# Two conditioned sequence blocks on one core: ranking, residual, last unit, DMA queue, and a product that starts on a copy of another in its PSUM bank

## The chip, the cores and the metric

The kernel runs on one core of a Trainium2 chip. The metric is device time in microseconds of one launch. The engines that matter are TensorE (PE in the profile), VectorE (DVE), ScalarE (ACT), GpSimd (POOL) and SyncE, whose queue (SPq) issues nearly all DMAs.

## The reference, cut to what matters

The input x is 32 batches of 64 tokens with 512 features, float32. Two layers follow each other; each is a block of attention and two MLPs, and then an adapter whose weights are chosen by the batch's role (one of three).

```python
attn = softmax(q @ k.T * 512**-0.5)            # q = x @ Wq, k = x @ Wk, per batch
attn_out = (attn @ v) @ Wp + bp                # v = x @ Wv
cms_out = gelu(attn_out @ cW1 + cb1) @ cW2 + cb2 + one_hot(code)      # first MLP, 512 -> 2048 -> 512
modifier = gelu(concat(attn_out, cms_out) @ mW1 + mb1) @ mW2 + mb2    # second MLP, 1024 -> 2048 -> 512
x = clip(x + cms_out + modifier, 0, 1)
u = gelu(x @ W_down[role] + b_down[role]) @ W_up[role] + b_up[role]    # adapter, 512 -> 256 -> 512
x = layernorm(x + u) * gamma[role] + beta[role]
```

## The kernel before

**Numbers.** Each float32 operand of a product is split into a high and a low part (ScalarE rounds the high part, VectorE subtracts it to get the low one) and a product is three matmuls (`product`, L543). "Split" below means this pair of operations; `h_hi`, `h_lo`, `s_lo` and the like are its semaphores.

**Passes.** Two halves of 16 batches (1024 tokens) times two layers are four passes p = 0 to 3. A pass is: attention for two blocks of 512 tokens, 16 units of MLP work (`mlps`: units 0 to 7 are the first MLP, 8 to 15 the second, each of 256 hidden features), and eight adapter tiles of 128 tokens. Every engine has its own program in a fixed order; semaphores tie them.

**The start.** The weights Wq Wk.T and Wv Wp of both layers are fused first: four products n = 0 to 3 in two sets of four PSUM banks, with `operands(n)` (split of the inputs) and `results(n)` (split of the product). Results are also stored to DRAM by SyncE, and `results(n)` on ScalarE waits for the store of n - 2 (`fuse_stored`) before it writes its buffer again. Between operands(1) and operands(2) VectorE runs `rank_batches` (L1177 on), some 40 tiny dependent steps that sort the batches so that tiles hold one role; SyncE waits for it (L340), reads the order from SBUF into registers and loads x batch by batch (`load_x`). Meanwhile GpSimd splits the bias rows in four operations on 4 x 2304 elements (L482 to L488).

**A unit** (`term`, `down`, `hidden`). Units 0 and 8 are plain: four blocks. The other 14 multiply 2 x 2 blocks with seven products P1 to P7. PE's order in unit u is P1, P5, P6, the down products of unit u - 1 for token block 0, P2, P7, the down products for block 1, P4, P3. P1 and P2 add up in `bank_a` (ps[0]), P6, P7 and P4 in `bank_b` (ps[1]), P5 and P3 in `bank_c`. ScalarE copies P1 to SBUF (`copy_p1`, L990), and VectorE adds it to what stands in bank_b after P6 (`make_u2`), after P7 (`make_z22`, which also adds P5) and after P4 (`make_z21`); `make_z12` adds P3. `hidden` takes the activation of the four results (H00, H10, H01, H11) in two ScalarE passes, and VectorE makes the low part. `add` (L1394) adds the down products to `acc`.

**The last unit** (15) also loads and splits the adapter's weights: `adapter_part` for down, `up_part` for up, in three roles each. VectorE's order ends: H11, up_part 0, up_part 1, z12, H01, the added token piece, the four `add` of block 0, adapter_part 2, clips.

**An adapter tile i.** VectorE clips acc (`clip`, two buffers xc), both engines split it, PE multiplies with the down weights and then turns the clipped tile into PSUM as the residual (both in `front`, the latter L803), after a wait for `normalise` of tile i - 3, since u_bank has three banks:

```python
for i in range(TILES):
    if i + 2 < TILES: r[i + 2] = front(p, half, i + 2)     # down product, then wait yn_done, then residual
    if i + 1 < TILES: turn_h(p, i + 1)
    if layer == 0 and 2 <= i < TILES - 1: turn_back(p, half, i - 2)
    adapter_up(p, half, i, r.pop(i))
```

VectorE's loop is: row_stats(i - 1), clip(i + 3), split_x(i + 3), normalise(i - 1), split_h(i + 1). GpSimd makes 1 / std (L523), then multiplies by gamma and adds beta (L526, L528). In layer 0, PE turns the tile back (`turn_back`, L840) for the next pass; in layer 1 SyncE stores it. SyncE's loop is: gains of tile i + 2 (two DMAs, each with a register load of the role), store of tile i (two DMAs, each with a register load of the batch), and between the halves three loads of x (each with a register load).

**Between passes.** Attention starts with four products per block (j = 0 to 3). Before a layer-1 pass, tile 5 is turned back ahead of them, tile 6 after j = 1, tile 7 after j = 3.

## Time and profile before

| | us |
|---|---|
| median of 3 runs | 2183.42 (2183.08 to 2183.86) |
| the profiled execution | 2183.24 |
| its span | 2181.4 |
| PE busy | 2094.2 (96%) |
| VectorE busy | 1417.4 (65%) |
| ScalarE busy | 864.6 (40%) |
| GpSimd busy | 378.1 (17%) |
| matmul weights loading (PEld) | 1729.3 |
| mean granted TensorE clock | 0.987 |

The table is read like this: the profiled execution is as long as the timed ones, so sums can be made against it. PE is nearly always busy, the others are not, and so the questions are where PE stands idle, who ends that, and where its clock is granted below 1.00.

### The profile page before, as it was taken

The numbers are of one execution on the slowest core, as the hardware profiler recorded it, in microseconds if no ns is written. First come the engines' busy times: TensorE is split into PE (matmuls) and PEld (weight loads), VectorE is DVE, ScalarE is ACT, GpSimd is POOL, SyncE is SP. The second block draws the span as 40 slices with busy tenths as digits, with TensorE's granted clock in tenths as the row PEclk, the third lists the DMA queues.
The fourth block names the chain that finished last, engine by engine and source line by source line (L and its number), as shares of the span: only waits on it lengthen the run. The fifth ranks groups of instructions, "written<-read, shape, count | busy, mean of one in ns | idle before, by whom it ended". The sixth has DMA issues, their size and how long they took to land.

```text
span 2181.4 us, 27070 instructions
## 1 busy us (share of the span) xinstructions
PE 2094.2 (96%) x9640; PEld 1729.3 (79%) x9640; DVE 1417.4 (65%) x2228; ACT 864.6 (40%) x1492; POOL 378.1 (17%) x348
## 2 busy tenths in 40 slices
PE   5999999999799999999889999999989999999996
PEld 4888888887688888888768888888867888888874
DVE  8577786557558777556646777765555777865563
ACT  4454453333245444333325444333324544433331
POOL 3011112210311102111130110212122111112204
PEclk8999999999999999999999999999999999999998
DMA  4501111223320121112451111111332012111123
GB/s 174 234 30 58 49 63 58 68 68 97 131 78 30 58 80 37 68 68 68 152 157 39 49 59 66 65 60 52 107 121 102 20 49 68 68 46 60 65 92 97
DMA packets 42402, 169.74 MB, mean 78 GB/s; under 512 B 5648, under 2 KB 9744, under 8 KB 34832
## 3 DMA queue, kind: packets, MB, share of 16 engines
q1 hardware_dynamic: 42272, 168.02, 22.7%
q8 instruction: 80, 1.31, 0.2%
q14 instruction: 50, 0.41, 0.1%
HBM read 146.99 MB, written 21.01 MB: 77 GB/s over the span
## 4 chain that ended last, share of the span: by engine, by line
PE 87%; DVE 6%; SPq 2%; issue 2%; ACT 1%; POOL 1%; DMA 1%; DVEq 0%; ACTq 0%; POOLq 0%
PE psum L543 80%; PE psum L828 1%; PE psum L640 1%; DVE acc L1394 1%; PE psum L618 1%; DVE yt L1541 1%; PE psum L803 1%; PE psum L795 1%; DVE xz L1146 1%; DVE stats L1526 1%; DVE fpart L1146 0%; ACT xz L1095 0%; DVE wup L1146 0%; PE psum L831 0%; POOL yt L526 0%
## 5 line engine op out<-in xcount | busy, mean ns | idle before, releaser
L543 PE MATMUL psum<-hs,wd 128*128 128x512 f32 x3072 | 718.2, 389 | 5.6 <-DVE acc L1394 5.6
L543 PEld LDWEIGHTS psum<-hs,wd 128*128 128x128 f32 x3072 | 576.1, 188 | 128.1 <-DVE acc L1394 7.3
L1394 DVE TENSOR_TENSOR acc<-psum,acc 128x512 f32<-128x512 f32 x448 | 291.0, 682 | 101.4 <-PE psum L543 101.2
L543 PE MATMUL psum<-cop,wsm 128*128 128x512 f32 x1416 | 354.7, 389 | 0.0
L543 PE MATMUL psum<-aop,wsm 128*128 128x512 f32 x1320 | 332.9, 389 | 0.0
L543 PE MATMUL psum<-aop,wsc 128*128 128x512 f32 x1320 | 310.7, 389 | 0.0
L543 PEld LDWEIGHTS psum<-cop,wsm 128*128 128x128 f32 x1416 | 265.8, 188 | 55.1
L543 PEld LDWEIGHTS psum<-aop,wsm 128*128 128x128 f32 x1320 | 247.8, 188 | 51.4
L543 PEld LDWEIGHTS psum<-aop,wsc 128*128 128x128 f32 x1320 | 247.5, 188 | 51.3
L1008 ACT ACTIVATE hs<-psum,bias 128x512 fp32r<-128x512 f32 x88 | 60.8, 691 | 445.4 <-PE psum L543 445.3
L1146 DVE TENSOR_TENSOR hs<-zt,hs 128x512 fp32r<-128x512 f32 x256 | 179.9, 703 | 85.5 <-ACT zt L1009 85.5
L1008 ACT ACTIVATE hs<-zt,bias 128x512 fp32r<-128x512 f32 x168 | 120.5, 717 | 229.1 <-DVE zt L1376 173.1
L1369 DVE TENSOR_TENSOR zt<-psum,zt 128x512 f32<-128x512 f32 x56 | 38.7, 692 | 184.5 <-PE psum L543 184.5
L1009 ACT ACTIVATE zt<-zt,bias 128x512 f32<-128x512 f32 x168 | 119.0, 708 | 0.0
L497 POOL TENSOR_TENSOR comb<-w1m 128x512 f32<-128x512 f32 x28 | 36.2, 1292 | 476.7 <-DMA w1m<-m_in 476.7
L1146 DVE TENSOR_TENSOR wsm<-w1m,wsm 128x512 fp32r<-128x512 f32 x156 | 107.9, 711 | 0.0
L543 PE MATMUL psum<-fw,xs 128*128 128x512 f32 x384 | 97.2, 406 | 4.7 <-DVE tq L1146 3.4
L978 ACT ACTIVATE wsm<-w1m 128x512 fp32r<-128x512 f32 x156 | 93.9, 623 | 3.7 <-POOL w1m L504 3.7
L501 POOL TENSOR_TENSOR comb<-comb,w1m 128x512 f32<-128x512 f32 x28 | 48.9, 1746 | 249.6 <-DVE wsm L1146 249.6
L497 POOL TENSOR_TENSOR comb<-w1c 128x256 f32<-128x256 f32 x28 | 20.7, 740 | 408.8 <-DMA w1c<-c_in 408.8
L543 PE MATMUL psum<-xs,fw 128*128 128x512 f32 x384 | 90.7, 395 | 0.4 <-DVE xs L1146 0.4
L543 PEld LDWEIGHTS psum<-fw,xs 128*128 128x128 f32 x384 | 73.1, 195 | 20.8 <-DVE tq L1146 3.9
(169 smaller groups left out, 2439.6 us busy)
## 6 DMA issues: line engine op xcount, KB each, us to landing
w1m<-m_in SPq DMA_DIRECT2D x32, 1024.0 KB, 4.9
w1c<-c_in SPq DMA_DIRECT2D x32, 512.0 KB, 3.5
w<-c_in SPq DMA_DIRECT2D x32, 512.0 KB, 3.5
w<-m_in SPq DMA_DIRECT2D x32, 512.0 KB, 3.5
gains<-roles_in SPq DMA_DIRECT2D x64, 256.0 KB, 3.6
fw<-fused SPq DMA_DIRECT2D x6, 2048.0 KB, 10.0
fused<-fw SPq DMA_DIRECT2D x4, 2048.0 KB, 8.2
xmid<-x SPq DMA_DIRECT2D x4, 2048.0 KB, 6.7
```

What stands on the lines that cost most here:

```text
L497: nc.gpsimd.tensor_tensor(st, w_block(u, 1, 0), w_block(u, 1, 1), ALU.add).then_inc(s1_made, 1)
L501: nc.gpsimd.tensor_tensor(st, st, w_block(u, 0, 0), ALU.subtract).then_inc(s2_made, 1)
L543: mm = nc.tensor.matmul(out, lhs(a), rhs(b), start=(start and n == 0), stop=(stop and n == total - 1), skip_group_check=reopened)
L618: nc.tensor.matmul(out, tq[:, j // 2, HI, j % 2, i * P:(i + 1) * P], xs[:, :, j, tile], start=(j == 0), stop=False)
L640: nc.tensor.matmul(out, val[:, HI, v_cols], val[:, :, p_cols], start=True, stop=False)
L795: nc.tensor.matmul(out, tokens, wdn_flat[:, bass.ds(role * (2 * KC * BN) + (c * KC + k) * BN, BN)], start=(b == 0 and k == 0 and a == c), ...
L978: nc.scalar.activation(slot(u, i)[:, HI, :], w_source(u, i), ACT.Copy).then_inc(s_hi[i], 1)
L1008: nc.scalar.activation(hs[:, b, HI, m, :], h_source(h, u), ACT.Gelu, bias=b1)
L1009: nc.scalar.activation(h_raw(h), h_source(h, u), ACT.Gelu, bias=b1).then_inc(h_hi[h], 1)
L1146: return nc.vector.tensor_tensor(out, a, hi.bitcast(F32), ALU.subtract)
L1369: nc.vector.tensor_tensor(zt[:, 2, :], bank_b()[:, :], zt[:, 0, :], ALU.add).then_inc(u3_done, 1)
L1394: nc.vector.tensor_tensor(dst, d_out[o][:, :], dst, ALU.add).then_inc(acc_done, 1)
```

## The change

It has five parts. (1) Start: the bias rows are laid out on 128 partitions and split in two operations instead of four; the ids are loaded from ScalarE's queue; ranking has 37 steps, of which ten run before operands(0) and 27 before operands(2); the one-hot table is made after results(3). (2) Adapter tiles: `residual` leaves `front` and runs behind turn_h of its own tile; the clip has a third buffer; tile 5 is turned back after attention's j = 0, tile 6 after j = 2. (3) Last unit: up_part 1 and 2 and the last adds move behind the first clips and splits. (4) SyncE: one gains DMA for a tile of one role; the order of the batches is read into registers once per half and kept. (5) In 7-product units ScalarE copies P1 into bank_b itself, P6 adds to it there, P4's result is read from bank_b directly; ScalarE copies P5 and the sum after P6 to SBUF; of VectorE's sums one before P4 and one after P3 remain. In the plain unit of the first MLP, H01 has bank ps[1] instead of ps[4].

The diff, cut to its core:

```diff
-RANKED = 40
+RANKED = 37
...
+        xct2 = at("xct2", [P, KC, P], F32, HS + 14)
...
-        xc = [xct[:, s, :, :] for s in range(2)]
+        xc = [xct[:, 0, :, :], xct[:, 1, :, :], xct2[:, :, :]]
...
-        back_bank = [ps[3], ps[4]] * (TILES // 2 - 1) + [ps[6], ps[7]]
+        back_bank = [ps[3], ps[4], ps[3], ps[4], ps[3], ps[6], ps[7], ps[6]]
...
-            return {H00: ps[0], H10: ps[6], H01: ps[1], H11: ps[7]} if kind else {H00: ps[2], H10: ps[3], H01: ps[4], H11: ps[5]}
+            return {H00: ps[0], H10: ps[6], H01: ps[1], H11: ps[7]} if kind else {H00: ps[2], H10: ps[3], H01: ps[1], H11: ps[5]}
...
-            return {H00: bank_a(), H11: zt[:, 2, :], H10: zt[:, 0, :], H01: zt[:, 1, :]}[h]
+            return {H00: bank_a(), H11: zt[:, 2, :], H10: bank_b(), H01: zt[:, 1, :]}[h]
...
-            sp.dma_start(ids[:, :], ids_in).then_inc(ids_loaded, 16)
...
-            def load_x(half, j):
-                sp.nop(nofuse=True)
-                r = sp.value_load(order[0:1, half * NB + j:half * NB + j + 1], min_val=0, max_val=BATCHES - 1)
+            def batch(half, j):
+                return sp.value_load(order[0:1, half * NB + j:half * NB + j + 1], min_val=0, max_val=BATCHES - 1)
+
+            def load_x(r, j):
                 sp.dma_start(x[:, j, :, :].rearrange("p k t -> p (k t)"),
                              x_in[bass.ds(r, 1)].rearrange("o p n -> (o p) n")).then_inc(x_loaded[j // (NB // 2)], 16)
 
             sp.wait_ge(ranked, RANKED)
+            sp.nop(nofuse=True)
+            where = []
             for j in range(NB):
-                load_x(0, j)
-            sp.wait_ge(rows_made, 4)
-            sp.dma_start(brows, rows[:, :].bitcast(F32)).then_inc(rows_stored, 16)
+                where.append(batch(0, j))
+                load_x(where[j], j)
+            sp.wait_ge(rows_made, 2)
+            for layer in range(LAYERS):
+                for part in range(2):
+                    half_rows = slice(layer * P // LAYERS, (layer + 1) * P // LAYERS)
...
-                for b in range(2):
+                pieces = 1 + general(half, i)
+                for b in range(pieces):
                     j = half * NB + 2 * i + b
                     r = sp.value_load(roles[0:1, j:j + 1], min_val=0, max_val=ROLES - 1)
-                    sp.dma_start(gains[b * SEQ:(b + 1) * SEQ, i % 2, :],
-                                 roles_in[layer, bass.ds(r, 1), BN + V:RP].to_broadcast([SEQ, 2 * V])).then_inc(gb_loaded[i % 2], 16)
-
-            def one_pass(half, layer):
+                    sp.dma_start(gains[b * P // pieces:(b + 1) * P // pieces, i % 2, :],
+                                 roles_in[layer, bass.ds(r, 1), BN + V:RP].to_broadcast([P // pieces, 2 * V])).then_inc(gb_loaded[i % 2], 16)
+
...
                 def store(i):
                     sp.wait_ge(b_done, 8 * p + i + 1)
                     for b in range(2):
-                        sp.nop(nofuse=True)
-                        j = half * NB + 2 * i + b
-                        r = sp.value_load(order[0:1, j:j + 1], min_val=0, max_val=BATCHES - 1)
-                        sp.dma_start(out[bass.ds(r, 1)].rearrange("o t v -> (o t) v"),
+                        sp.dma_start(out[bass.ds(where[2 * i + b], 1)].rearrange("o t v -> (o t) v"),
                                      yt[b * SEQ:(b + 1) * SEQ, i % 4, :]).then_inc(stored[i % 4], 16)
 
                 if layer:
...
+            one_pass(0, 0, where, None)
+            sp.nop(nofuse=True)
+            after = [batch(1, j) for j in range(NB)]
+            one_pass(0, 1, where, after)
+            one_pass(1, 0, after, None)
+            one_pass(1, 1, after, None)
...
-            nc.gpsimd.tensor_copy(rows_hi[:, :], rows_raw[:, :]).then_inc(rows_made, 1)
+            nc.gpsimd.tensor_copy(rows[:, HI, :], rows_raw[:, :]).then_inc(rows_made, 1)
             pool.wait_ge(rows_made, 1)
-            pool.wait_ge(ranked, 3)
-            nc.gpsimd.tensor_scalar(rows_part[:, :], rows_hi[:, :].bitcast(F32), rc[0:2 * LAYERS, 1:2], None, ALU.mult).then_inc(rows_made, 1)
-            nc.gpsimd.tensor_scalar(rows_raw[:, :], rows_raw[:, :], rc[0:2 * LAYERS, 0:1], None, ALU.mult).then_inc(rows_made, 1)
-            pool.wait_ge(rows_made, 3)
-            nc.gpsimd.tensor_tensor(rows[:, :], rows_raw[:, :], rows_part[:, :], ALU.add).then_inc(rows_made, 1)
+            nc.gpsimd.tensor_tensor(rows[:, LO, :], rows_raw[:, :], rows[:, HI, :].bitcast(F32), ALU.subtract).then_inc(rows_made, 1)
 
...
-                    if b == 0 and layer == 1 and j in (1, 2):
-                        pe.wait_ge(x_back, 8 * half + 4 + j)
+                    if b == 0 and layer == 1 and j == 1:
+                        pe.wait_ge(x_back, 8 * half + TILES - 3)
...
-                    if b == 0 and layer == 1 and j % 2:
-                        turn_back(p - 1, half, TILES - 2 + j // 2)
+                    if b == 0 and layer == 1 and j != 1:
+                        turn_back(p - 1, half, TILES - 4 + max(j, 1))
...
-                        pe.wait_ge(z21_done, strassen(p, u))
+                        pe.wait_ge(h_hi[H10], n)
...
-                    if i == P6:
-                        if u == NG + 1:
-                            pe.wait_ge(h_hi[H01], n)
-                        elif u % NG > 1:
-                            pe.wait_ge(z21_done, e)
                 if not first:
-                    if i == P2:
+                    if i in (P6, P2):
                         pe.wait_ge(p1_copied, e + 1)
                     if i == P7:
-                        pe.wait_ge(u2_done, e + 1)
+                        pe.wait_ge(u2_copied, e + 1)
                     if i == P4:
-                        pe.wait_ge(u3_done, e + 1)
+                        pe.wait_ge(z22_done, e + 1)
                     if i == P3:
-                        pe.wait_ge(z22_done, e + 1)
+                        pe.wait_ge(p5_copied, e + 1)
...
+
+            def residual(p, i):
+                if i == 2:
+                    pe.wait_ge(acc_done, 8 * UNITS * (p + 1))
                 if i >= 3:
-                    pe.wait_ge(yn_done, e - 2)
+                    pe.wait_ge(yn_done, 8 * p + i - 2)
                 for k in range(KC):
-                    mm = nc.tensor.matmul(u_bank[i % 3][:, k * P:(k + 1) * P], xc[s][:, k, :], ident[:, :], start=(k == 0), stop=False,
+                    mm = nc.tensor.matmul(u_bank[i % 3][:, k * P:(k + 1) * P], xc[i % 3][:, k, :], ident[:, :], start=(k == 0), stop=False,
                                           is_transpose=True)
                 mm.then_inc(tr_done, 1)
-                return r
 
...
                 pe.wait_ge(hg_done, e + 1)
                 if i == 0:
-                    pe.wait_ge(acc_done, 8 * UNITS * (p + 1))
+                    pe.wait_ge(acc_done, 8 * UNITS * (p + 1) - 3)
...
-                    r = {i: front(p, half, i) for i in range(2)}
+                    r = {0: front(p, half, 0)}
+                    residual(p, 0)
+                    r[1] = front(p, half, 1)
                     turn_h(p, 0)
                     for i in range(TILES):
                         if i + 2 < TILES:
                             r[i + 2] = front(p, half, i + 2)
                         if i + 1 < TILES:
                             turn_h(p, i + 1)
+                            residual(p, i + 1)
                         if layer == 0 and 2 <= i < TILES - 1:
                             turn_back(p, half, i - 2)
                         adapter_up(p, half, i, r.pop(i))
-                    if layer == 0:
-                        turn_back(p, half, TILES - 3)
...
+            act.dma_start(ids[:, :], ids_in).then_inc(ids_loaded, 16)
...
             def copy_p1(p, u):
+
                 act.wait_ge(prod[P1], strassen(p, u) + 1)
-                act.wait_ge(h_lo[H10], UNITS * p + u)
-                nc.scalar.activation(zt[:, 0, :], bank_a()[:, :], ACT.Copy).then_inc(p1_copied, 1)
+                act.wait_ge(h_hi[H01 if plain(u - 1) else H10], UNITS * p + u)
+                nc.scalar.activation(bank_b()[:, :], bank_a()[:, :], ACT.Copy).then_inc(p1_copied, 1)
+
+            def copy_p5(p, u):
+                act.wait_ge(prod[P5], strassen(p, u) + 1)
+                act.wait_ge(h_lo[H11], UNITS * p + u)
+                nc.scalar.activation(zt[:, 2, :], bank_c(u)[:, :], ACT.Copy).then_inc(p5_copied, 1)
+
+            def copy_u2(p, u):
+                act.wait_ge(prod[P6], strassen(p, u) + 1)
+                act.wait_ge(h_lo[H01], UNITS * p + u)
+                nc.scalar.activation(zt[:, 1, :], bank_b()[:, :], ACT.Copy).then_inc(u2_copied, 1)
 
...
+                elif h == H10:
+                    act.wait_ge(prod[P4], strassen(p, u) + 1)
+                    act.wait_ge(h_lo[H10], n)
                 else:
-                    act.wait_ge({H11: z22_done, H10: z21_done, H01: z12_done}[h], strassen(p, u) + 1)
+                    act.wait_ge({H11: z22_done, H01: z12_done}[h], strassen(p, u) + 1)
...
                 hidden(p, layer, u, H01)
                 hidden(p, layer, u, H11)
+                if kind == 0:
+                    copy_p1(p, u + 1)
                 weight_part(p, u + 1, P2)
+                if kind:
+                    copy_p1(p, u + 1)
                 op_part(p, kind, P7)
                 weight_part(p, u + 1, P7)
...
-                    copy_p1(p, u)
+                    copy_p5(p, u)
                     for i in (P4, P3):
                         weight_part(p, u, i)
+                    copy_u2(p, u)
...
                         up_part(p, 0)
-                        up_part(p, 1)
+                    if nxt and not plain(u + 1):
+                        copy_p1(p, u + 1)
                     hidden(p, layer, u, H01)
 
...
                     split_x(0)
-                    up_part(p, 2)
+                    up_part(p, 1)
                     split_x(1)
                     gelu_h(0)
                     split_x(2)
+                    up_part(p, 2)
                     gelu_h(1)
                     split_h(0)
...
+            compare_batches()
             operands(0)
             operands(1)
-
-            assert rank_batches() == RANKED
+            place_batches()
+            assert done == RANKED
+            operands(2)
+            results(0)
+            operands(3)
+            results(1)
+            results(2)
...
+            for k in range(KC):
+                split_block(0, 0, k)
+            results(3)
             dve.wait_ge(consts_in, 16)
             for layer in range(LAYERS):
...
-                e = strassen(p, u)
-                dve.wait_ge(p1_copied, e + 1)
-                dve.wait_ge(prod[P6], e + 1)
-                dve.wait_ge(h_lo[H01], UNITS * p + u)
-                nc.vector.tensor_tensor(zt[:, 1, :], bank_b()[:, :], zt[:, 0, :], ALU.add).then_inc(u2_done, 1)
-
             def make_z22(p, u):
                 e = strassen(p, u)
                 dve.wait_ge(prod[P7], e + 1)
-                dve.wait_ge(h_lo[H11], UNITS * p + u)
-                nc.vector.tensor_tensor(zt[:, 2, :], bank_b()[:, :], zt[:, 0, :], ALU.add).then_inc(u3_done, 1)
-                dve.wait_ge(prod[P5], e + 1)
-                dve.wait_ge(u3_done, e + 1)
-                nc.vector.tensor_tensor(zt[:, 2, :], bank_c(u)[:, :], zt[:, 2, :], ALU.add).then_inc(z22_done, 1)
-
-            def make_z21(p, u):
-                dve.wait_ge(prod[P4], strassen(p, u) + 1)
-                nc.vector.tensor_tensor(zt[:, 0, :], bank_b()[:, :], zt[:, 0, :], ALU.add).then_inc(z21_done, 1)
+                dve.wait_ge(p5_copied, e + 1)
+                nc.vector.tensor_tensor(zt[:, 2, :], bank_b()[:, :], zt[:, 2, :], ALU.add).then_inc(z22_done, 1)
 
             def make_z12(p, u):
                 dve.wait_ge(prod[P3], strassen(p, u) + 1)
-                dve.wait_ge(u2_done, strassen(p, u) + 1)
+                dve.wait_ge(u2_copied, strassen(p, u) + 1)
                 nc.vector.tensor_tensor(zt[:, 1, :], bank_c(u)[:, :], zt[:, 1, :], ALU.add).then_inc(z12_done, 1)
...
                     def clip(i):
-                        if i >= 2:
-                            dve.wait_ge(tr_done, 8 * p + i - 1)
-                        nc.vector.tensor_scalar(xc[i % 2], acc[:, :, i * P:(i + 1) * P], 0.0, 1.0, ALU.max, ALU.min).then_inc(xc_done, 1)
+                        if i >= 3:
+                            dve.wait_ge(tr_done, 8 * p + i - 2)
+                        nc.vector.tensor_scalar(xc[i % 3], acc[:, :, i * P:(i + 1) * P], 0.0, 1.0, ALU.max, ALU.min).then_inc(xc_done, 1)
...
                     add(p, layer, last, 0, *range(KC))
-                    adapter_part(p, 2)
                     dve.wait_ge(xadd_done, NG * (p + 1))
                     dve.wait_ge(acc_done, 8 * UNITS * (p + 1) - 4)
                     clip(0)
+                    adapter_part(p, 2)
+                    split_x(0)
                     clip(1)
-                    split_x(0)
-                    up_part(p, 2)
+                    up_part(p, 1)
                     add(p, layer, last, 1, 0)
                     split_x(1)
-                    add(p, layer, last, 1, 1, 2, 3)
+                    dve.wait_ge(dn_done, 8 * UNITS * (p + 1))
                     clip(2)
                     split_x(2)
+                    up_part(p, 2)
                     split_h(0)
+                    add(p, layer, last, 1, 1, 2, 3)
                     for i in range(TILES):
                         if i == TILES - 2:
```

## Rows read from the trace of the kernel before

**Rows 1.** Waits of PE: who waited for whom, us in total, times, longest.
```profile
PE psum L803 <- DVE yt L1541: 30.5, 18, 1.9
PE psum L543 <- DVE fw L1146: 20.9, 1, 20.9
```

**Rows 2.** Windows: busy us per engine, clock, DMA; MLPs of pass 0.
```profile
134.60:527.80 393.20, 393.20 (x1735) 325.63 (x1735) 265.95 (x399) 160.87 (x273) 61.13 (x54) 1.00 0.19 63
```

**Rows 3.** Timeline, start: start us, us, engine, line, operation, out<-in, count.
```profile
21.81 6.11 POOL L485 TENSOR_SCALAR rows_part<-rows_hi,rc 4x2304 f32<-4x2304 f32 x1 [1.88 <-DVE rk L1199]
21.90 6.06 DVE L1203 TENSOR_SCALAR rk<-idf 128x32 f32<-128x32 f32 x1
...
28.02 5.59 DVE L1206 TENSOR_TENSOR rk<-rk 128x32 f32<-128x32 f32 x1
...
45.53 17.34 SPq L342 DMA_DIRECT2D x<-x_in  x16
46.18 4.48 DVE L1146 TENSOR_TENSOR fpart<-fraw,fpart 128x2048 fp32r<-128x2048 f32 x2
...
51.41 23.77 PE L543 MATMUL psum<-fpart 128*128 128x512 f32 x96 [20.89 <-DVE fw L1146]
...
63.33 15.88 SPq L352 DMA_DIRECT2D fused<-fw  x4
70.85 2.07 ACT L882 ACTIVATE fw<-psum 128x512 fp32r<-128x512 f32 x4 [34.64 <-DMA fused<-fw]
...
75.02 11.04 PE L543 MATMUL psum<-xs,fw 128*128 128x512 f32 x48
```

**Rows 4.** Timeline, last unit of pass 0 on VectorE and PE.
```profile
531.11 2.36 DVE L1146 TENSOR_TENSOR wup<-raw_u,wup 128x1024 fp32r<-128x1024 f32 x2 [0.18 <-ACT wup L1042]
...
537.54 5.74 PE L543 MATMUL psum<-hs,wd 128*128 128x512 f32 x24 [1.40 <-DVE acc L1394]
```

**Rows 5.** Timeline, adapter tiles of pass 0.
```profile
558.12 2.65 PE L828 MATMUL psum<-wup,hz 128*128 x6
...
568.08 0.70 DVE L1526 BATCH_NORM_STATS2 stats<-psum 128x6 f32<-128x512 f32 x1 [1.42 <-PE psum L831]
...
569.17 0.42 DVE L1504 TENSOR_SCALAR xct<-acc 128x512 f32<-128x512 f32 x1
...
571.75 0.66 PE L803 MATMUL psum<-ident,xct 128*128 128x128 f32 x4 [1.77 <-DVE yt L1541]
...
572.82 1.64 PE L828 MATMUL psum<-wup,hz 128*128 x6
...
573.19 1.30 POOL L528 TENSOR_TENSOR yt<-yt,gains 128x512 f32<-128x512 f32 x1
...
574.92 0.70 DVE L1526 BATCH_NORM_STATS2 stats<-psum 128x6 f32<-128x512 f32 x1 [1.41 <-PE psum L831]
```

**Rows 6.** Timeline, entries into pass 1 and pass 2.
```profile
591.45 4.62 DVE L1146 TENSOR_TENSOR xs<-x,xs 128x512 fp32r<-128x512 f32 x4
...
594.98 1.11 PE L840 MATMUL psum<-ident,yt 128*128 128x128 f32 x4 [2.69 <-POOL yt L528]
...
1128.03 5.49 PE L543 MATMUL psum<-fw,xs 128*128 128x512 f32 x12 [3.45 <-DVE tq L1146]
```

**Rows 7.** Timeline of SyncE's DMA queue, adapter tiles of pass 1.
```profile
1109.74 1.84 SPq L358 DMA_DIRECT2D gains<-roles_in  x2
...
1118.38 1.83 SPq L358 DMA_DIRECT2D gains<-roles_in  x2
```

**Rows 8.** Line L341 alone: ns (min/median/max), first to last start.
```profile
L341 SPq TENSOR_LOAD <-order x32: 263/269/471, 44.6 to 1131.9; - x32
```

**Rows 9.** Timeline, units 1 and 3 of pass 0.
```profile
148.19 0.73 ACT L1009 ACTIVATE zt<-psum,bias 128x512 f32<-128x512 f32 x1
...
149.50 5.60 PE L543 MATMUL psum<-hs,wd 128*128 128x512 f32 x24
...
190.75 0.58 ACT L990 ACTIVATE zt<-psum 128x512 f32<-128x512 f32 x1
```

116 lines of the change are left out of this document (53 added, 63 removed).

## The prediction

> **What bounds the kernel now.** I read the page first: PE is busy 96% of a span of 2181.4 us. I then asked who keeps PE waiting. Two causes carry most of its 87 us of idle time: the product L803 (the residual turned into PSUM) waits for VectorE's normalise, 18 times and 30.5 us, and once PE waits 20.9 us at the start [rows 1]. The window table shows the other side: the 393.2 us of MLP products of one pass hold no idle PE, and they come four times [rows 2]. So nothing is to be won in the products, and anything that opens a wait there is paid in full; the gains lie at the start, in the last unit, in the adapter tiles and where one pass hands over to the next.
>
> **The change part by part.**
>
> **Start.** VectorE ranks the batches from 21.0 to 44.5 us. Three of its tiny steps there last as long as a GpSimd operation on 4 x 2304 elements beside them: 6.06 us beside 6.11, then 5.59, and a third alike [rows 3]. The change makes these operations 128 x 36, moves ten of the steps ahead of the first split, into time in which VectorE waits, and leaves 27 steps of about 0.2 us, 5.5 us. The ids go out on ScalarE's queue, so the first weights start 0.4 us earlier. Then: first splits end at 20.6, ranking 26.1, two operand splits of 2.24 us [rows 3] 30.6, first result split 31.3. PE, done with its second weight product at 30.1, waits 1.2 us, not 20.9. Its next 96 products take 21.8 us at full clock (23.8 before [rows 3], the first of them slow) and end at 53.2. What is late next is the DMA queue: 16 loads of x at 1.12 us each [rows 3] run from 26.2 to 44.2, the first product is stored from 45 (63.3 before), and ScalarE, which waits for that store, goes on 7.5 us after its issue, as before [rows 3]: 52.6. With its results (2.1 us) and the first split of x, attention starts at 56.2; before it started at 75.0 [rows 3]. That is 18.9 us. I take off 0.7, because PE stands 3 us ahead of it and a similar stand cost the next product 1.1 us (below): **-18.2**, between -16.5 and -19.5.
>
> **Last unit.** VectorE splits two thirds of the up weights, 2.36 us, ahead of the last sum, and PE then waits 1.40 us for the first added output [rows 4]. One of them (1.2 us) now comes later, in a place where PE still has 5 us of products. The wait falls to 0.25: 4 x 1.15 = **-4.6**.
>
> **Adapter tiles.** One tile of layer 0 takes 6.84 us, from statistics to statistics (568.08 to 574.92). In it VectorE does statistics, clip, split and normalise, and only then may PE do the residual, after 1.77 us of waiting [rows 5], and behind it turn h and the up product, on which the next statistics hang. The change moves the residual behind turn h, lets it wait for the tile before, and gives the clip a third buffer. PE's own work is 6.84 - 1.77 = 5.07 us a tile (4.6 in layer 1, which lacks the turn back's 0.45), and VectorE's 4.1: the 3.7 from the statistics to PE's start, and the split of h, 0.4. So all 18 waits go: -30.5; the four small waits of the third front, 0.4 each: -1.8. The first of these waits each time leaves PE slow, six up products in 2.65 us instead of 1.64 [rows 5]; four such stretches together lose 6.3 us: -6.3. What is late next: a ring GpSimd add, clip, ScalarE split, VectorE split, normalise, GpSimd multiply, add. From the clip's start to PE's, behind the normalise, it is 2.6 us (569.17 to 571.75), and GpSimd's multiply and add take 1.3 each [rows 5]. If the clip can't run beside the add, as the ranking steps couldn't [rows 3], the ring takes 2.6 + 2 x 1.3 + some 0.15 between them = 5.35 us, more than PE's 5.07 or 4.6; over the five tiles with a clip PE then loses 0.3 in layer 0 and 1.0 in layer 1. With 0.25 for the first split of each pass: +3.6. Sum **-35.0**, between -31 (the ring costs 1.5 a pass more) and -38 (no ring).
> The Trainium skill, SBUF - State Buffer, section on the two sides of SBUF's ports, says that VectorE (with two SBUF inputs or in its two-port modes) and GpSimd hold one port pair for a whole instruction and the loser stops; the 6.06 us beside 6.11 agree. By it the ring is real, and it is in the sum.
>
> **Handing over.** Into pass 1 PE waits 2.69 us for tile 5's turn back and runs slow after it, about 1.5 us more [rows 6]. The turn back now goes behind the first attention product. Late next is VectorE's split of x, which takes 4.62 us for four beside GpSimd [rows 6]: it ends some 2 us after PE is free. Net -2.3; into pass 3, -1.2. Into pass 2 the DMA queue is the trouble: a tile costs it 8.6 us [rows 7], against 4.6 + 1.8 = 6.4 for a tile, so gains and stores run late and PE waits 3.45 us, then runs 12 products in 5.49 us instead of 2.75 [rows 6], and two more waits follow: 8.2 us of waits and 4.8 of slow products. A tile now has one gains DMA (1.26), two stores without the 0.27 us register load and what belongs to it [rows 8] (1.3) and three loads (1.4), 4.1 us with its waits, below the tile's 4.6 to 5.3; the same split costs 2.3. Net -10.7, but -7 if the queue is still late. The 32 register loads are done ahead; the second 16, 10 us, stand behind the last gains of pass 0 and end before x is back. Sum **-14.2**, -9 to -17.
>
> **End.** The last two stores without register loads: **-1.3**. The last three tiles otherwise run on GpSimd's ring of 4.2 us each, which the change doesn't touch.
>
> **The sixth product.** In 7-product units P6 now starts on the copy of P1, so it waits for ScalarE; the three sums on VectorE that go are under PE already and give nothing. In the window of P5 (6 matmuls, 1.36 us, in the units of the first MLP; 12 and 2.72 in those of the second) ScalarE must start (0.2 after P1) and copy. A copy from PSUM to SBUF takes 0.58 [rows 9]; no row shows one that ends in PSUM. At 0.58 there are 0.5 us to spare. H10's activation, read straight from PSUM, moves forward, the copy goes ahead of H01, and H01, which is delayed by 1.2 us, isn't read for 12 us. One unit is different: unit 1. ScalarE works off its backlog until 148.9 [rows 9], while P6 would start 1.36 ahead of the down products, at 148.14. The copy ends at 149.4: a wait of 1.3 us in each pass, **+5.1**. From below, 0 (the backlog is shorter); from above, a copy of twice 0.58 adds 0.1 us in 24 units and 0.6 in unit 1, 5 us more. I take 5.1, by the copy row.
> The Trainium skill, ScalarE: Activation LUTs, says that ScalarE writes to PSUM faster than to SBUF. By it the copy would be under 0.58 and the wait in unit 1 a little shorter. No row shows it.
>
> **Sum.** -18.2 - 4.6 - 35.0 - 14.2 - 1.3 + 5.1 = -68.2. The profiled execution took 2183.24 us (span 2181.4, 1.8 around it), 0.2 below the median of the runs. So 2183.24 - 68.2 = **2115.0**.
>
> **Rivals.** *Easier than thought*: no ring and no wait in unit 1, 2115 - 3.3 - 5.1 = 2106.6. For it: GpSimd's multiply and add leave a small gap in which the clip may slip. Against: ScalarE's backlog is in the rows. *The queue stays late*: pass 1 still runs at SP's pace, and the split of x waits; +4 to +9, 2119 to 2124. For it: 4.1 us is built from pieces. Against: it would have to be 30% off. *P6 waits everywhere*: the copy takes over 1.1 us, so that all 28 units of the first kind wait some 0.5 more: +14, 2129. For it: an unseen form. Against: every 128x512 operation of ScalarE lies at 0.6 to 0.7. *Slower than before*: the same mechanism, where the copy outlasts P5 also in the second kind. With 68 us to eat in 56 units it must wait 1.2 us more in each, that is a copy of some 2.5 us; it decides only from there. *The change doesn't do what it says*: the clip still waits for the residual that reads its buffer, so the residual wait stays; then 2115 + 38 = 2153. Against: with three buffers clip i + 3 waits for residual i, one tile earlier.
>
> **How the numbers follow.** Forecast 0.60; easier 0.16; queue late 0.12; P6 everywhere 0.07; wait stays 0.03; slower 0.02. The range goes down to 2105 and up to 2128, which takes in the first three and the bounds of the start and the ring. What the measurement can tell from no change is about 0.2%, 4 us; none of the cases but the last comes near, so faster 0.97, same 0.01, slower 0.02.
>
> **What would show it.** Right: in the waits of PE the row L803 from VectorE's normalise is gone or under 3 us, the wait for the fused weights at the start near 1.2, attention at 56; a new row for P6 with ScalarE's copy, 4 times and about 1.3 each; tiles 5.1 and 4.6 to 5.3 us apart; SP's groups about 4 us. Wrong: an idle PE within the 393 us stretches beyond unit 1; a clip or x split of VectorE that takes more than 1 us in each tile; granted clock under 1.00 in the adapters.

## The result, and the profile after

The changed kernel takes **2111.0 us** (2110.4 to 2112.6) against 2183.6 for the kernel before: 0.9666 of its time, 95% interval 0.9649 to 0.9682. 2115.0 had been predicted, between 2105 and 2128. The profiled execution took 2110.7 us, its span is 2109.0: 72.4 us less than before where 68.2 were forecast. What follows asks where each of these came from, since terms can be wrong and cancel.

First the page of the kernel after (engine, busy us, share, instructions), then its waits of PE (who waited for whom, us in total, times, longest).

```profile
span 2109.0 us, 26689 instructions
PE 2080.5 (99%) x9640; PEld 1719.5 (82%) x9640; DVE 1302.2 (62%) x2057; ACT 920.9 (44%) x1604; POOL 358.4 (17%) x346
```
```profile
PE psum L551 <- DVE xs L1174: 5.6, 4, 4.0
PE psum L551 <- issue: 4.8, 4, 1.2
PE psum L551 <- DVE acc L1404: 1.8, 4, 0.5
...
PE psum L798 <- DVE xz L1174: 1.2, 4, 0.3
PE psum L847 <- POOL yt L536: 0.8, 1, 0.8
```

Idle PE fell from 87 us to 28.5, which includes small gaps that have no row. Both causes of [rows 1] are gone: no product waits for the normalise, and none for the fused weights. What is new is in the second row: 4 waits of 1.2 us "issue", the sixth product of unit 1 once in each pass.

The table below needs marks. Two cut each pass: **S**, attention's first score product, and **T**, the first product of the adapters. Their rows in pass 0 and the next S:

```profile
70.27 0.28 PE L626 MATMUL psum<-xs,tq 128*128 128x256 f32 x1
...
525.13 1.59 PE L798 MATMUL psum<-wdn,xz 128*128 x12
...
580.75 0.28 PE L626 MATMUL psum<-xs,tq 128*128 128x256 f32 x1
```

Read off in each kernel's trace in the same way (the last up product is taken with the bias product behind it, and to its end):

| us | before | after | difference |
|---|---|---|---|
| start to first S | 88.62 | 70.27 | -18.35 |
| S to T, passes 0 to 3 | 454.50, 454.53, 461.11, 454.54 | 454.86, 454.86, 454.89, 454.88 | +0.36, +0.33, -6.22, +0.34 |
| T to the next S or the end | 68.33, 67.34, 68.81, 63.62 | 55.62, 52.50, 58.01, 53.11 | -12.71, -14.84, -10.80, -10.51 |
| of that, T to the last up product | 49.17, 47.04, 52.34, 49.92 | 39.92, 36.91, 42.90, 40.58 | -9.25, -10.13, -9.44, -9.34 |

### The profile page after: what moved, and what is told of

It is laid out like the page before. It is cut to its first block, busy times and chain, and to the rows that moved or that the text cites. A ratio compares the mean times of both kernels' runs of the same rounds, so it can differ in the third digit from the quotient of the medians.

```text
span 2109.0 us, 26689 instructions
## 1 busy us (share of the span) xinstructions
PE 2080.5 (99%) x9640; PEld 1719.5 (82%) x9640; DVE 1302.2 (62%) x2057; ACT 920.9 (44%) x1604; POOL 358.4 (17%) x346
## 3 DMA queue, kind: packets, MB, share of 16 engines
q1 hardware_dynamic: 42096, 167.97, 23.1%
q8 instruction: 80, 1.31, 0.3%
## 4 chain that ended last, share of the span: by engine, by line
PE 92%; DVE 3%; issue 1%; SPq 1%; ACT 1%; DMA 1%; POOL 1%; ACTq 0%; DVEq 0%; POOLq 0%
PE psum L551 84%; PE psum L798 2%; PE psum L835 1%; PE psum L626 1%; PE psum L648 1%; DVE acc L1404 0%; DVE xs L1174 0%; PE psum L838 0%; ACT wup L1069 0%; PE psum L649 0%; PE psum L628 0%; PE psum L823 0%; PE psum L811 0%; SPq L333 0%; DMA fraw<-fuse_in 0%
## 5 line engine op out<-in xcount | busy, mean ns | idle before, releaser
L551 PEld LDWEIGHTS psum<-cop,wsm 128*128 128x128 f32 x1416 | 265.8, 188 | 55.2
L1031 ACT ACTIVATE hs<-psum,bias 128x512 fp32r<-128x512 f32 x144 | 98.6, 684 | 401.9 <-PE psum L551 401.8
L1031 ACT ACTIVATE hs<-zt,bias 128x512 fp32r<-128x512 f32 x112 | 81.0, 723 | 91.1 <-PE psum L551 80.2
L1032 ACT ACTIVATE zt<-psum,bias 128x512 f32<-128x512 f32 x144 | 98.1, 681 | 0.0
L551 PEld LDWEIGHTS psum<-xs,fw 128*128 128x128 f32 x384 | 72.1, 191 | 22.9 <-issue 5.2
```

The lines of the kernel that those rows point to most:

```text
L551: mm = nc.tensor.matmul(out, lhs(a), rhs(b), start=(start and n == 0), stop=(stop and n == total - 1), skip_group_check=reopened)
L1031: nc.scalar.activation(hs[:, b, HI, m, :], h_source(h, u), ACT.Gelu, bias=b1)
L1032: nc.scalar.activation(h_raw(h), h_source(h, u), ACT.Gelu, bias=b1).then_inc(h_hi[h], 1)
```

## The experiments

Unless said otherwise the edits are made in the changed kernel, so 2111.0 is what they stand against.

**The start, shape alone.** The kernel before, with only the rows' work in the form 128 x 36:

```diff
-rows_raw = at("rows_raw", [2 * LAYERS, BROW], F32, CO + 32)
+rows_raw = at("rows_raw", [P, RW], F32, CO + 32)
```


> The kernel before with one part of the change: GpSimd's work on the rows of the adapters in the form 128 x 36 instead of 4 x 2304, and what hangs on it. Theory (three tiny VectorE steps each last as long as a GpSimd operation beside them, 6.06, 5.59 and a third alike, and would take 0.2 to 0.7): the ranking ends 16.5 us earlier and attention with it, nearly the whole gain of the start: 2183.6 - 16 = 2167.6. Rival (the steps moved ahead of the first split carry the gain): 2183.6 - 4 = 2179 or less.

Measured: 2166.6 us (2164.7 to 2169.6), first S at 72.05 (88.62 before), so 16.6 of the start's 18.35 us are this edit. With the shape it takes two of the four operations away and the wait of GpSimd for the ranking; the three go together and weren't taken apart. The timeline shows why it helps: GpSimd is done before VectorE's steps begin; the same steps stand in [rows 3] with 6.06 and 5.59 us:

```profile
17.98 0.76 POOL L487 TENSOR_TENSOR rows<-rows_raw,rows 128x36 fp32r<-128x36 f32 x1
...
20.11 0.24 DVE L1202 TENSOR_SCALAR rk<-idf 128x32 f32<-128x32 f32 x1
...
20.53 0.19 DVE L1205 TENSOR_TENSOR rk<-rk 128x32 f32<-128x32 f32 x1
```

**The start, what is late next.** In the changed kernel ScalarE stands 16.29 us for the store of the first product, PE then 4.01 for x, and PE runs its 48 products in 12.73 us:

```profile
44.50 15.06 SPq L364 DMA_DIRECT2D fused<-fw  x4
...
51.12 2.06 ACT L890 ACTIVATE fw<-psum 128x512 fp32r<-128x512 f32 x4 [16.29 <-DMA fused<-fw]
...
54.98 12.73 PE L551 MATMUL psum<-xs,fw 128*128 128x512 f32 x48 [4.01 <-DVE xs L1174]
```
```diff
                 load_x(where[j], j)
+                if j == 7:
+                    store_fused(0)
+            store_fused(1)
             sp.wait_ge(rows_made, 2)
```


> The changed kernel with the first product stored after 8 of the 16 loads of x and the second after all 16, ahead of the brows. Theory (ScalarE's split of x stands behind a store that stands behind 16 loads): ScalarE goes on at about 39 instead of 51.1, PE's wait of 4.01 us ahead of the attention goes, and since PE doesn't stand, the 48 attention products take 10.9 us instead of 12.7: 2111.0 - 4.0 - 1.8 = 2105.2. Rival (x itself is late, since its second half is issued 1 to 2 us later): the wait only moves to another place and the time is within 1.5 us of 2111.0.

Measured: 2104.8 us, first S at 64.28, that is 6.0 earlier. The store is issued at 32.64 between the halves of x, and the attention follows without a wait and without slow products:

```profile
32.64 0.43 SPq L354 DMA_DIRECT2D fused<-fw  x1
...
50.68 11.04 PE L557 MATMUL psum<-xs,fw 128*128 128x512 f32 x48
```

**The sixth product's wait.** In unit 1 ScalarE makes both activations of H11 (129.28 to 130.42) ahead of the copy:

```profile
130.42 0.64 ACT L1000 ACTIVATE psum<-psum 128x512 f32<-128x512 f32 x1
...
131.16 1.63 PE L551 MATMUL psum<-aop,wsc 128*128 128x512 f32 x6 [1.21 <-issue]
```
```diff
                 hidden(p, layer, u, H01)
+                if kind == 0:
+                    copy_p1(p, u + 1)
                 hidden(p, layer, u, H11)
-                if kind == 0:
-                    copy_p1(p, u + 1)
```


> The changed kernel with one move: in the first unit of the first kind ScalarE copies P1 right after the activation of H01, ahead of that of H11. Theory (ScalarE's backlog makes P6 of unit 1 wait): the copy now starts at 129.28 instead of 130.42 and ends before P6 wants to start at 129.95, so the four waits of 1.21 us go: 2111.0 - 4.8 = 2106.2. Rival (what stands behind the copy becomes late: H11's activation and the weight product behind it come 0.6 us later): a new wait takes the place of the old one and the time stays between 2109 and 2111.

Measured: 2107.0 us. The wait falls from 1.21 to 0.23 each and S to T from 454.86 to 453.89, 4 x 0.97 = 3.9 us. The theory holds, but for the 0.2 us that are left of each wait.

**The last part of the change undone.** All 7-product units go back to the sums of the kernel before:

```diff
-                first = i in (P1, P5) and which == 0
+                first = i in (P1, P5, P6) and which == 0
-                    if i in (P6, P2):
+                    if i == P2:
                         pe.wait_ge(p1_copied, e + 1)
```
and with it the copy to SBUF and VectorE's three more sums.

> The changed kernel without its last part: P6 opens its bank itself, P1 is copied to SBUF, and VectorE makes the three sums that the change had dropped. Everything else as in the changed kernel. Theory (that part only costs, the four waits of P6 in unit 1): 2111.0 - 4.8 = 2106.2. Rival (the sums that VectorE no longer makes help elsewhere, in the last unit above all, where the wait for the first added output is 0.5 us and would go back towards 1.4): 2108 to 2111. Rival (they help more than the wait costs): above 2111.

Measured: 2105.4 us, 5.6 under the changed kernel. S to T is 453.41, 453.39, 453.39, 453.37: this part of the change costs 1.47 us a pass. 1.21 of it is the wait in unit 1; and the last unit's wait is 0.30 here, 0.44 to 0.47 with the part:

```profile
518.79 5.78 PE L551 MATMUL psum<-hs,wd 128*128 128x512 f32 x24 [0.30 <-DVE acc L1403]
```

So the sums that VectorE is spared bring nothing, not even there. Since this kernel and the one before make these sums in the same way, the two also give the last unit alone: 454.50 - 453.41 = 1.1 us a pass, which is the fall of its wait from 1.40 to 0.30.

**How much room the copy has.**

```diff
+                nc.scalar.activation(bank_b()[:, :], bank_a()[:, :], ACT.Copy).then_inc(p1_first, 1)
+                act.wait_ge(p1_first, strassen(p, u) + 1)
                 nc.scalar.activation(bank_b()[:, :], bank_a()[:, :], ACT.Copy).then_inc(p1_copied, 1)
```


> The changed kernel with ScalarE's copy of P1 made twice, one after the other. P1's copy starts some 0.2 us after P1 and takes 0.58; P5 covers 1.36. Theory (0.5 us are spare in the units of the first kind): a second copy, 0.58 and 0.1 between them, exceeds that by 0.1 in 24 units and is paid in full, 0.7, in unit 1: 2111.0 + 2.4 + 2.8 = 2116. Rival (nothing is spare, P6 rides on the copy everywhere): 0.7 in 28 units, 2111 + 19.6 = 2131. Rival (ScalarE has more room): unit 1 alone, 2114.

Measured: 2122.7 us, between the theory and its rival, from two executions that lie 3 us apart (2121.2 and 2124.2, the profiled one). S to T grew by 2.4 us a pass (4.0 in pass 2). Of it 0.6 is unit 1, where the wait became 1.81. The second copy starts 0.62 us after the first, and the sixth product's first matmul at 154.91:

```profile
153.57 0.58 ACT L1001 ACTIVATE psum<-psum 128x512 f32<-128x512 f32 x1 [0.28 <-PE psum L552]
154.19 0.58 ACT L1003 ACTIVATE psum<-psum 128x512 f32<-128x512 f32 x1
...
154.91 0.47 PE L552 MATMUL psum<-aop,wsc 128*128 128x512 f32 x1
...
149.29 7.24 PE L552 MATMUL psum<-aop,wsc 128*128 128x512 f32 x30
```
In the changed kernel the same 30 products take 6.96 us:
```profile
146.24 6.96 PE L551 MATMUL psum<-aop,wsc 128*128 128x512 f32 x30
```
0.62 us more of copy cost 0.28 of PE in such a unit. Six such units and unit 1 make 6 x 0.28 + 0.6 = 2.3 a pass, which is what was seen. But the cost is not the overrun: in the trace that first matmul starts 0.41 us behind the last one of P5, where 0.23 is the usual distance, so it is late by 0.18, and the one behind it comes after 0.31 and not 0.23. The copy outlasts its room by 0.18, and the room is 0.62 - 0.18 = 0.44 us.

The 1.6 us more in pass 2 are PE's clock. Behind the wait of 1.81 in unit 1, from 1157.8 to 1161.3, the granted clock was at the lower level; in passes 0, 1 and 3 it stayed at 1.00 behind the same wait. The window (from:to, length, PE busy, granted clock, DMA share, GB/s):
```profile
1158.00:1160.00 2.00, 2.00 (x6) 0.50 0.00 0
```
The profiled execution also lost 2.4 us ahead of the first S (72.71 against 70.27), where the copy has no part; these are not the edit's.

**The order of the residual.**

```diff
                             r[i + 2] = front(p, half, i + 2)
+                            residual(p, i + 2)
                         if i + 1 < TILES:
                             turn_h(p, i + 1)
-                            residual(p, i + 1)
```


> The changed kernel with TensorE's residual back ahead of turn h (right behind the front of its own tile), three clip buffers kept. Theory (the order is what removed the 18 waits for the normalise and the slow up products behind them): waits and slow stretches come back, 30.5 + 1.8 + 6.3 less some 3 of wait for the sums: 2111 + 35 to 38 = 2146 to 2149. Rival (the third clip buffer did it, the order is indifferent): within 4 us of 2111.

Measured: 2155.8 us, 44.8 more than the changed kernel and some 7 more than the upper end of what was expected. 18 waits for the normalise are back, 27.4 us, with four of 1.0 for the last sums, and slow products behind them (six up products in 2.23 and 2.71 us instead of 1.63):

```profile
540.86 0.66 PE L811 MATMUL psum<-ident,xct 128*128 128x128 f32 x4 [1.80 <-DVE yt L1548]
...
541.49 2.23 PE L835 MATMUL psum<-wup,hz 128*128 x6
...
550.18 2.71 PE L835 MATMUL psum<-wup,hz 128*128 x6
```
T to the next S is 68.01, 64.75, 67.69, 63.39. In all but the second of them that is within 1.2 us of the kernel before, and T to the last up product is even 0.2 to 1.7 us longer than there: without the new order the rest of the change wins nothing in the tiles.

**Two clip buffers in the new order.**

```diff
-                        if i >= 3:
-                            dve.wait_ge(tr_done, 8 * p + i - 2)
-                        nc.vector.tensor_scalar(xc[i % 3], ...
+                        if i >= 2:
+                            dve.wait_ge(tr_done, 8 * p + i - 1)
+                        nc.vector.tensor_scalar(xc[i % 2], ...
```


> The changed kernel with the clip back in two buffers, new order kept, so that clip i + 2 waits for the residual of tile i. Theory (from the trace of the changed kernel: the residual of tile i ends at 541.7 where the clip now starts at 540.1, but there the clip runs 0.96 to 1.31 us beside GpSimd's add instead of 0.42): the clip starts 1.6 us later and takes 0.5 less, the front has 1.3 us to spare in layer 0 and 1.0 in layer 1, so PE loses nothing in layer 0 and 0.1 to 0.2 a tile in layer 1: 2111 + 1 to 3 = 2112 to 2114. Rival (the third buffer carries the gain: with two the residual wait stays, which was put at +38): about 2149.

Measured: 2123.8 us. Both were wrong: the third buffer is worth 12.8 us, neither 2 nor 38. T to the next S grew by 2.7, 3.8, 2.5 and 3.4 us. VectorE works in order, and the clip now holds it for 1.0 to 1.8 us in five of a pass's eight tiles; the split and the normalise stand behind it, and with the normalise GpSimd's work and the turn back:

```profile
538.40 0.43 DVE L1510 TENSOR_SCALAR xct<-acc 128x512 f32<-128x512 f32 x1 [1.76 <-PE psum L811]
...
540.62 1.69 PE L798 MATMUL psum<-wdn,xz 128*128 x12 [0.53 <-DVE xz L1174]
...
543.77 0.66 PE L847 MATMUL psum<-ident,yt 128*128 128x128 f32 x4 [0.35 <-POOL yt L536]
```
My expectation had only asked whether the front gets its split in time in a tile that begins on time. It left out that the delay is carried from tile to tile.

**A longer ring.**

```diff
+                        nc.gpsimd.tensor_tensor(yt[:, i % 4, 0:RING], yt[:, i % 4, 0:RING], gains[:, s, 0:RING], ALU.mult)...
                         nc.gpsimd.tensor_tensor(y[i % 4], y[i % 4], gains[:, s, V:2 * V], ALU.add).then_inc(b_done, 1)
```


> The changed kernel with one more GpSimd operation of 128x256 in each tile, between its multiply and its add (the output is multiplied once too often in half of its columns). It makes the ring add, clip, split, normalise, multiply 0.75 to 0.85 us longer: 5.18 + 0.8 = 6.0 us a tile against PE's 5.01. Theory (the ring is there, but the front stands 1.3 to 1.6 us ahead of its need and uses that up first): tiles stay 5.01 and 4.55 apart for one or two tiles, then go to 6.0; together 3.5 a pass in layer 0, 4.5 in layer 1 and some 6 at the entries and the end, 2111 + 22 = 2133. Rival, the step of the prediction (each excess of the ring is paid from the first tile on): 1.0 and 1.4 us in each of five tiles, 4 x 6 = 24 and the same 6: 2141. Rival (no ring, GpSimd is beside the path): only the end grows, 2111 + 3 to 5 = 2115.

Measured: 2125.3 us, +14.2. T to the next S grew by 3.6, 3.7, 2.5 and 3.2 us, and pass 2's S to T by 1.3. So GpSimd is not beside the path; but no 1.0 us a tile was lost. In layer 0 of the changed kernel GpSimd's multiplies start 5.17 to 5.18 us apart, and the clip is stretched beside its add (0.96 to 1.31 us). Here they start 5.45 apart, and the clip takes 0.42 to 0.67. First the changed kernel, then this one:

```profile
543.32 1.28 POOL L534 TENSOR_TENSOR yt<-yt,gains 128x512 f32<-128x512 f32 x1 [1.84 <-DVE yt L1547]
...
548.50 1.28 POOL L534 TENSOR_TENSOR yt<-yt,gains 128x512 f32<-128x512 f32 x1 [1.85 <-DVE yt L1547]
...
549.86 1.28 POOL L536 TENSOR_TENSOR yt<-yt,gains 128x512 f32<-128x512 f32 x1
550.12 1.31 DVE L1510 TENSOR_SCALAR xct<-acc 128x512 f32<-128x512 f32 x1
```
```profile
540.25 0.42 DVE L1514 TENSOR_SCALAR xct<-acc 128x512 f32<-128x512 f32 x1
...
540.44 1.36 POOL L540 TENSOR_TENSOR yt<-yt,gains 128x512 f32<-128x512 f32 x1
...
543.75 1.27 POOL L536 TENSOR_TENSOR yt<-yt,gains 128x512 f32<-128x512 f32 x1 [0.99 <-DVE yt L1551]
...
549.20 1.28 POOL L536 TENSOR_TENSOR yt<-yt,gains 128x512 f32<-128x512 f32 x1 [0.99 <-DVE yt L1551]
...
552.75 0.66 PE L851 MATMUL psum<-ident,yt 128*128 128x128 f32 x4 [0.24 <-POOL yt L540]
```
With the added operation the clip slips in ahead of the add, and the ring is GpSimd's own: power 1.0, VectorE's normalise 0.8, multiply, extra, add. Where PE meets it in layer 0 is the turn back, not the residual. In layer 1, which has no turn back, it is the split of the last tile (0.86 us, both passes) and in pass 1 turn h (1.85). Of my three cases none has the size; the one with some slack comes nearest.

**The DMA queue as before.**

```diff
-                pieces = 1 + general(half, i)
+                pieces = 2
-                        sp.dma_start(out[bass.ds(where[2 * i + b], 1)]...
+                        sp.nop(nofuse=True)
+                        sp.dma_start(out[bass.ds(batch(half, 2 * i + b), 1)]...
```


> The changed kernel with the DMA queue's work as before: two gains DMAs a tile in every tile, and a register load ahead of each store and each load of x. Theory (8.6 us of queue a tile against tiles of 4.55 us: the faster tiles make the old queue worse than it was, since all the time the tiles gave in pass 1 is taken back by the queue): pass 1 takes 15 us more up to its MLP, the end 2, the start 1: 2111 + 18 = 2129. Rival (the parts add as in the prediction, where the queue was worth 8.4 into pass 2 and 1.3 at the end): 2121.

Measured: 2134.1 us, +23.1, past the theory's end. Pass 1 from T to S takes 66.39 us, against 52.50 in the changed kernel and 67.34 before; pass 2 from S to T 461.35, as before (461.11); the end 2.8 more. The queue's groups are 8.6 to 9.0 us apart, and PE waits for what comes through them, 4.34 and 4.82 us at a time:

```profile
1060.17 1.81 SPq L369 DMA_DIRECT2D gains<-roles_in  x2
...
1068.77 2.19 SPq L369 DMA_DIRECT2D gains<-roles_in  x2
```
```profile
1078.92 12.51 PE L549 MATMUL psum<-xs,fw 128*128 128x512 f32 x48 [4.34 <-DVE xs L1172]
1096.25 5.49 PE L549 MATMUL psum<-fw,xs 128*128 128x512 f32 x12 [4.82 <-DVE tq L1172]
```
So in pass 1 the old queue takes back nearly all that the faster tiles give: 66.39 us against 67.34 in the kernel before. The other way round is in the run with the residual's old order, which has the new queue: there T to S of pass 1 is 64.75 (2.6 under the kernel before) and pass 2's S to T 454.87 (6.2 under it). With the old tiles the new queue is thus worth some 9 us here, with the new tiles 13.9 + 6.5 = 20.4. The tiles' gain in pass 1 needs the queue's, the queue's doesn't need the tiles', and one must not add what each gives alone.

**The end.** The last two tiles' multiply and add on VectorE, the last gains in a place of their own:

```diff
+                    if at_end(p, TILES - 2):
+                        scale_and_shift(TILES - 2)
                     normalise(TILES - 1)
+                    if at_end(p, TILES - 1):
+                        scale_and_shift(TILES - 1)
```


> The changed kernel with the last two tiles of the last pass multiplied by the gains and shifted on VectorE instead of GpSimd, and the last tile's gains in a place of their own. Theory (the end hangs on GpSimd's 4.2 us a tile and on a DMA of gains issued late): the last add ends at 101.5 - 105.5 relative to now, that is 4 us earlier: 2107.0. Rival (only the 1.76 us wait for the gains goes): 2109.2.

Measured: 2108.0 us. The last add starts at 2101.90 on VectorE, where it was at 2104.27 on GpSimd; with its 0.69 instead of 1.26 us it ends 2.94 earlier. The fourth microsecond was wrongly counted: the last statistics stand behind the normalise of tile 6, and that waits for GpSimd's 1 / std, which stands behind GpSimd's add of tile 5.

```profile
2097.12 0.81 DVE L1558 TENSOR_SCALAR yt<-psum,mv,rstd 128x512 f32<-128x512 f32 x1 [2.32 <-POOL rstd L540]
...
2101.90 0.69 DVE L1566 TENSOR_TENSOR yt<-yt,gains_end 128x512 f32<-128x512 f32 x1
```

**Together.** The three edits in one kernel (the stores, the copy, the end):

> The three edits of this call together in the changed kernel: P1's copy ahead of H11, the stores ahead, the last two tiles on VectorE. Theory (the three lie in different places of the chain and add): 2111.0 - 4.8 - 5.8 - 4.0 = 2096.4. Rival (one of them is taken up by the next late thing): 2099 to 2104.

Measured: 2098.2 us (2098.0 to 2098.4), 0.9603 of the time before (0.9590 to 0.9616). The parts gave 6.2, 4.0 and 3.0 alone, 13.2 in sum, and 12.8 together: they add, to 0.4 us. 14.6 had been expected; 1.4 of the difference lies in the parts' own sizes.

> The stores ahead and the last two tiles on VectorE, as before, and in place of the move of P1's copy the whole seven-product scheme of the kernel before (P6 opens its bank, P1 copied to SBUF, three more sums on VectorE). Theory (from S to T0, attention's scores to the first adapter product, a pass took 453.9 us with the copy moved and 453.4 with the old scheme, so P6 on the copy costs 0.5 a pass even with its wait mended): 2098.2 - 2.0 = 2096.2. Rival (the two fall together once the wait in unit 1 is gone): within 0.7 of 2098.2.

Measured: 2096.3 us (2096.3 to 2096.8), 0.9598 (0.9585 to 0.9611). It is the kernel with the stores ahead, the end on VectorE, and the change's last part taken out in place of the moved copy: the fastest of all the kernels here.

## Why the prediction was right, point by point

| term | forecast | measured | from |
|---|---|---|---|
| start | -18.2 | -18.35 | first S |
| last unit | -4.6 | -4.4 | S to T, with the old sums |
| adapter tiles | -35.0 | -38.2 | T to the last up product |
| handing over | -14.2 | -16.1 | the rest of T to S, and pass 2's S to T |
| end | -1.3 | -1.2 | the rest of the last T to the end |
| sixth product | +5.1 | +5.9 | 4 x 1.47 |
| sum | -68.2 | -72.4 | |

**The start**: the size is right, its inside less so. The ranking takes 5.5 us from 18.2 to 23.7, as worked out. PE's wait for its second weight product, put at 1.2, is not there, since the first loads came earlier in this execution (the first weight product starts at 6.79 us, and the first two products' operands are split by 18.2 instead of 20.6). The queue is what is late next, as said: 44.5 for the store, 51.1 for ScalarE (45 and 52.6 forecast), attention at 54.98 (56.2). But PE then stands 4.0 us, not 3, and what that costs is 1.7 us of slow products (12.73 against 11.04 in [rows 3]), not 0.7. Two errors of 1 us cancel, which is luck.

**The last unit**: right, to 0.2 us. It was not taken out alone; the figure is the difference of two kernels' S to T, and the wait in the trace agrees.

**The adapter tiles**: the mechanism is right and two sizes were off. All 18 waits and the four of the third front are gone, the tiles are 5.01 and 4.55 us apart, inside the forecast, and the clock is 1.00 in them. The term came out 3.2 us better than forecast. 1.8 of that is the slow products: PE's busy time from T to the last up product fell by 1.9, 2.1, 2.0 and 2.1 us, 8.1 together, where 6.3 was put down. The other 1.4 is what the ring costs.

In layer 0 the ring is there: 5.18 us where 5.35 was worked out, with three clips of 0.96, 1.14 and 1.31 us in each of its passes. Each of them ends 0.3 us behind GpSimd's add, however late it began beside it, and alone a clip takes 0.42. That is the two-port rule (the Trainium skill, SBUF — State Buffer, section SBUF: two separate sides: one of the two engines stops for as long as the other holds the pair; the rows agree). Two of these clips are over the 1 us that the prediction had named as a sign of being wrong (it asked for it in each tile), and they still cost next to nothing. In layer 1, where a tile of PE is 0.46 us shorter, only the first is stretched. The other two start ahead of the add, take 0.42, and it is the add that becomes longer:

```profile
1055.13 0.42 DVE L1510 TENSOR_SCALAR xct<-acc 128x512 f32<-128x512 f32 x1
...
1055.18 1.50 POOL L536 TENSOR_TENSOR yt<-yt,gains 128x512 f32<-128x512 f32 x1
```

The multiplies there are 5.18, 4.82 and 4.68 us apart. This is the slip that the *easier* rival had asked for. With it layer 1, which was to pay most, shows one wait of 0.23 us and no more.

In layer 0 the order doesn't slip, and the step of the prediction that was off is how the ring reaches PE. It let PE pay in each pass (0.3 us in layer 0, 1.0 in layer 1, 2.6 in all), as if its next product hung on the normalise just made. It doesn't: the residual needs the bank of three tiles before, the turn back the sum of two tiles before (at 541.55 it is 0.77 us behind that sum), and the split of x is 1.1 to 1.5 us ahead of PE. Three gaps of 5.18 - 5.01 take 0.5 us of that, and it shows once, in a turn back that waits 0.77 us at the end of pass 0's tiles.

The recorded figures don't follow from each other, either: 5.35 against 5.07 and 4.6 over five tiles would be 1.4 and 3.8 us a pass, so that something was taken off without being named; 1.5 us more in each pass gives -29 as the upper bound, not -31; and *easier* takes off 3.3 for a ring that stands in the sum with 2.6. None of this moves the total out of its range, but the ring's 2.6 stands somewhere between 0 and the 10.3 of its own rows, without a reason for the place.

**Handing over**: into pass 1 -3.5 (forecast -2.3), into pass 2 -11.3 (-10.7), into pass 3 -1.4 (-1.2). The queue's share was tested above; what the moved turn backs give was not taken out alone, and is argued from the wait of 2.69 us in [rows 6] that is gone. The queue issues a tile's group in 3.3 us after its register load (1057.49 to 1060.76), within the 4.1 worked out, and then waits for the tile; it no longer sets the pace. The split of x, feared at 2 us behind PE, held it for 0.30 at the first entry and 0.58 and 0.72 at the second: it takes 4.69 us as before, but its first pieces are ready in time, and PE needs them one after the other. The queue's group, then the split and PE behind it at the first entry:

```profile
1057.49 0.33 SPq L371 DMA_DIRECT2D gains<-roles_in  x1
...
1059.24 1.52 SPq L347 DMA_DIRECT2D x<-x_in  x3
```
```profile
562.79 4.69 DVE L1174 TENSOR_TENSOR xs<-x,xs 128x512 fp32r<-128x512 f32 x4
...
566.93 1.67 PE L551 MATMUL psum<-xs,fw 128*128 128x512 f32 x6 [0.30 <-DVE xs L1174]
```

**The sixth product**: right in kind and place. The wait is where the backlog of ScalarE put it, 1.21 us against 1.3, four times, and nowhere else; moving the copy ahead of two activations takes it down to 0.23. The other 0.26 us a pass the sum didn't have; most of it is the last unit's wait, which is 0.44 to 0.47 us with the copy into the bank and 0.30 without. The room in the other units is 0.44 us where 0.5 was worked out, so the rival *P6 waits everywhere* begins at a copy of 1.0 us, not 1.1. And being late costs more than the lateness: 0.18 late cost 0.28 in a unit. The Trainium skill, ScalarE: Activation LUTs, section Step-by-step: what each stage is for, has ScalarE write to PSUM faster than to SBUF; here the two forms differ by 8 ns in the median:

```profile
L1000 ACT ACTIVATE psum<-psum x56: 582/582/644, 130.4 to 2017.2; 128x512 f32<-128x512 f32 x56
L1005 ACT ACTIVATE zt<-psum x56: 575/590/601, 133.2 to 2019.9; 128x512 f32<-128x512 f32 x56
```
(ns, min/median/max; the first copies to PSUM, the second to SBUF.)

**The rival that the wait stays** was priced at 38 us for a clip that waits for its own residual. Two buffers in the new order are the nearest thing to it, and cost 12.8; the old order with three buffers costs 44.8. The two don't add up to what the tiles gained, since either one alone holds the others up; the old order with two buffers was not run on top of the rest of the change.

## What to carry to other kernels

When a ring of several engines is a little slower than the engine that sets the end, count for how many tiles it runs and how far ahead each hand-over stands before charging the excess: 0.17 us in each of three gaps met 0.77 us of slack at the tightest hand-over, and all that was seen of it is one wait behind the last of these tiles. And a delay isn't judged in one tile: an in-order engine carries what it waits for from tile to tile, as the two clip buffers showed. A part that frees an engine which isn't on the path is worth nothing and may still open a wait; here the copy of P1 into the bank cost 5.6 us, and taking it out is part of the fastest kernel.

## What the runs showed of the hardware

More work on GpSimd took time off a VectorE operation: with one more 128x256 operation a tile the clip ran in 0.42 to 0.67 us ahead of the add instead of 0.96 to 1.31 beside it, because the two met in another order (the split behind it went from 0.69 to 0.98). The changed kernel shows the same in its own layer 1: 0.42 us for the clip, 1.50 instead of 1.28 for the add.

4.0 us of standing cost 1.7 us more behind them: the changed kernel's first attention products ran at the lower of PE's two clock levels (1.2 instead of 2.4 GHz) for 3.4 us, from 55.2 to 58.6, those of the kernel with the early store at full clock throughout. 3.4 us at half speed are the 1.7. A stand of 1.8 us can cost as much, as pass 2 of the doubled copy showed, or nothing, as its other passes did. The windows of both (from:to, length, PE busy, granted clock, DMA share, GB/s):

```profile
55.00:56.00 1.00, 1.00 (x3) 0.60 0.62 262
56.00:58.00 2.00, 2.00 (x6) 0.50 1.20 508
58.00:60.00 2.00, 2.00 (x9) 0.85 0.97 401
```
```profile
50.00:52.00 2.00, 2.00 (x10) 1.00 0.94 354
```
